# First expert stage of a small vision tower in slots of 64, as products on 64x64 quarters of TensorE

## The reference

```python
h = tokenizer(x)                                  # shifted patches, layer norm, one product
h = h + attention(layernorm(h))                   # 12 heads, quantised
h = h + ffn0(layernorm(h))                        # this stage is changed
h = h + ssm_block(layernorm(h))
h = h + ffn1(layernorm(h))                        # top 2 of 8 experts, hidden 768
```

```python
route = softmax(x @ router_w + router_b); e = argmax(route)
out[token] = (silu(x @ w1[e]) * (x @ w2[e])) @ w3[e]      # w1, w2: 192 x 512, w3: 512 x 192
out = out.astype(bfloat16) * max(route)
```

## Time and profile before

| quantity | value |
|---|---|
| median of 3 runs | 405.71 us |
| time of the profiled execution | 409.78 us |
| its span, first to last instruction | 408.0 us |
| mean granted clock of TensorE in it | 0.903 of 2.4 GHz |
| busy: PE, weight load, DVE, ACT, POOL | 85%, 71%, 45%, 33%, 26% |
| PE pieces of the first expert stage on the chain | 119.5 to 180.2 us |

### The profile page before, as it was taken

How to read it: one execution, slowest core, us unless ns; L and a number is a source line. 1 busy time by engine, 2 the same in 40 slices (tenths; PEclk the granted TensorE clock), 3 DMA queues, 4 the chain that set the end, 5 groups by cost and what they waited for, 6 DMA issues and landing times.

```text
span 408.0 us, 7081 instructions
## 1 busy us (share of the span) xinstructions
PE 348.6 (85%) x2758; PEld 291.5 (71%) x2758; DVE 184.0 (45%) x474; ACT 134.8 (33%) x278; POOL 104.5 (26%) x133
## 2 busy tenths in 40 slices
PE   4999946989788999966896987888899999999970
PEld 1999923567667999962465654575799999999960
DVE  2786793996552222216398555266422212121213
ACT  2997311444303222321387042321321212121210
POOL 3299542000023443122032202000423232211120
PEclk9999976987776999996999798995999999999995
DMA  7933239930371795007003999002249999999204
GB/s 237 345 84 75 63 81 253 271 93 2 108 202 52 203 247 124 15 16 195 0 0 77 258 252 259 28 0 67 60 105 291 277 254 255 258 251 249 65 31 130
DMA packets 28707, 59.51 MB, mean 146 GB/s; under 512 B 10081, under 2 KB 15234, under 8 KB 28674
## 3 DMA queue, kind: packets, MB, share of 16 engines
q1 hardware_dynamic: 26274, 53.48, 50.1%
q0 software_dynamic: 2400, 5.57, 5.0%
HBM read 55.12 MB, written 3.92 MB: 145 GB/s over the span
## 4 chain that ended last, share of the span: by engine, by line
PE 60%; DVE 17%; ACT 8%; DMA 8%; issue 4%; SPq 2%; POOL 0%; DVEq 0%; POOLq 0%; ACTq 0%
PE ps L1604 15%; PE ps L1629 12%; PE ps L1616 9%; PE ps L1412 4%; PE ps L1345 4%; DMA xw<-in_xw 3%; DVE cv L1264 3%; ACT xp L661 2%; PE ps L1418 2%; DVE xn L974 2%; DVE xn L950 2%; PE ps L1467 2%; SPq L349 2%; PE ps L1547 2%; DMA yg<-token_y 2%
## 5 line engine op out<-in xcount | busy, mean ns | idle before, releaser
L1604 PE MATMUL ps<-xgt,wup 128*128 128x128 f32 x576 | 70.9, 280 | 2.3 <-DVE ht L1196 1.8
L1604 PEld LDWEIGHTS ps<-xgt,wup 128*128 128x128 f32 x576 | 69.4, 196 | 2.8 <-issue 2.8
L1196 DVE TENSOR_TENSOR ht<-sg,ps 128x384 f32<-128x384 f32 (+1 forms) x56 | 27.7, 497 | 77.5 <-ACT sg L774 75.5
L597 POOL DMA_INDIRECT xg<-token_x,src_id x26 | 25.3, 972 | 145.5 <-DVE src_id L1166 95.3
L1629 PE MATMUL ps<-wdn,ht 128*128 128x192 f32 x288 | 53.8, 335 | 0.0
L1345 PE MATMUL ps<-busy 128*128 128x512 bf16 x108 | 38.9, 486 | 11.1 <-DVE h L1211 6.6
L1629 PEld LDWEIGHTS ps<-wdn,ht 128*128 128x128 f32 x288 | 46.1, 190 | 3.1
L604 POOL DMA_INDIRECT token_y<-ysb,row_id x28 | 27.5, 981 | 67.6 <-ACT ysb L781 67.6
L774 ACT ACTIVATE sg<-ps 128x384 f32<-128x384 f32 (+1 forms) x56 | 24.8, 444 | 49.9 <-PE ps L1616 49.1
L1353 PE MATMUL ps<-weff,xp 128*128 128x193 f32 x240 | 39.9, 327 | 1.6 <-ACT xp L661 1.6
L1353 PEld LDWEIGHTS ps<-weff,xp 128*128 128x128 f32 x240 | 39.2, 190 | 2.4 <-issue 2.4
(11 more groups left out here) (295 smaller groups left out, 511.0 us busy)
## 6 DMA issues: line engine op xcount, KB each, us to landing
wup<-in_m_w SPq DMA_DIRECT2D x16, 576.0 KB, 8.5
wup<-in_m_w SPq DMA_DIRECT2D x48, 192.0 KB, 9.4
wdn<-in_m_w SPq DMA_DIRECT2D x16, 576.0 KB, 11.4
wup<-in_m_w SPq DMA_DIRECT2D x12, 384.0 KB, 6.1
wup<-in_m_w SPq DMA_DIRECT2D x36, 128.0 KB, 6.6
wdn<-in_m_w SPq DMA_DIRECT2D x12, 384.0 KB, 9.3
xw<-in_xw SPq DMA_DIRECT2D x2, 784.0 KB, 12.3
wall<-in_w_sh SPq DMA_DIRECT2D x2, 768.0 KB, 10.2
```

Source lines behind the costliest of these rows:

```text
L597: g.indirect_dma_start(xg[:, j, :], None, token_x[m], bass.IndirectOffsetOnAxis(ap=src_id[:, j:j + 1], axis=0))\
L1196: v.tensor_tensor(ht[:, j % 2, s, 0:half], sg[:, s, 0:half], ps[:, 2 * s + 1, 0:half], ALU.mult)\
L1604: mm(ps[:, 2 * s + g, c * P:c * P + P], up[:, col:col + P], xgt[:, 0, j * P:j * P + P], start=(c == 0), stop=False)
```

## The change

The first expert stage now works in halves of 64 slots. An expert owns one half at least, and 16 halves (`M1_HALVES`) hold any routing: 8 static and 8 looked up. Two halves make one tile of 128 slots for the gather and the scatter, so there are 8 gathers' worth of tiles (`M1_TILES` is now 8) and 8 scatters. Weights are loaded for each half, so 16 times and not 12.

All products of the stage use 64x64 quarters of the array: the row half (partitions 0 to 63 or 64 to 127 of the operands) holds the gate matrix `w1` or the up matrix `w2`, the column half (partitions of the output) one of two blocks of 64 hidden units. For this the 192 channels stand as three blocks of 64 in both halves of the partitions (`xh`), and the weight buffer holds `w1` in partitions 0 to 63 and `w2` in 64 to 127. `across` transposes with 12 products of 64x64, `up_half` has 48 products for a half, `down_pair` 16 over 192 columns for both halves of a tile. The two row halves of `down_pair` write separate banks; ACT copies one to `y_low` and DVE adds the other (`both_rows`).

The weight loads are cut differently. `expert_weights` issues seven transfers: two that fill all 128 partitions from both matrices at once, through a source view that steps first over the matrix (g, two of them) and then over 64 rows, four pieces of 32 rows with 512 floats, and the down matrix as before.

```diff
+H = 64
+M1_HALVES = (T + E * (H - 1)) // H
+M1_TILES = (M1_HALVES + 1) // 2
+KB = D // H
-W_LOADS = 5
+W_LOADS = (7, 5)
...
+        y_low = sb("y_low", [P, D], scope=arena)
+        xh = xgt[:].rearrange("p m n -> p (m n)")[:, 0:2 * M1_TILES * D].rearrange("p (t k n) -> p t k n", k=KB, n=H)
...
-                sp.dma_start(up[0:DH, 0:2 * hid], w12[:, 0, :]).then_inc(S[f"d_wb{b}"], 16)
-                sp.dma_start(up[DH:P, 0:2 * hid], w12[0:lo, 1, :]).then_inc(S[f"d_wb{b}"], 16)
-                sp.dma_start(up[0:REM, 2 * hid:3 * hid], w12[lo:DH, 1, 0:hid]).then_inc(S[f"d_wb{b}"], 16)
-                sp.dma_start(up[REM:P, 2 * hid:3 * hid], w12[lo:DH, 1, hid:2 * hid]).then_inc(S[f"d_wb{b}"], 16)
+                if m == 0:
+                    def both(k):
+                        return up[:, k * hid:(k + 1) * hid]
+
+                    def gate_and_up(half, rows):
+                        return w12[rows, half, :].rearrange("p (g n) -> g p n", g=2)
+
+                    pieces = [(both(0), gate_and_up(0, slice(0, H))), (both(2), gate_and_up(1, slice(lo, DH)))]
+                    for g in range(2):
+                        at = H * g
+                        pieces += [(up[at:at + DH - H, hid:2 * hid], w12[H:DH, 0, g * hid:(g + 1) * hid]),
+                                   (up[at + DH - H:at + H, hid:2 * hid], w12[0:lo, 1, g * hid:(g + 1) * hid])]
...
+                for dst, src in pieces:
+                    sp.dma_start(dst, src).then_inc(S[f"d_wb{b}"], 16)
                 sp.dma_start(down[:], w3).then_inc(S[f"d_wb{b}"], 16)
...
-                for j in range(first, r["n"]):
+                for j in range(first, M1_HALVES if m == 0 else r["n"]):
                     if j == E:
                         sp.wait_ge(S["v_te"], m + 1)
-                    sp.wait_ge(S["p_y"], j - r["bufs"] + 1 + r["before"])
+                    last = j - r["bufs"]
+                    sp.wait_ge(S["p_y"], (last // 2 if m == 0 else last) + 1 + r["before"])
...
+                def both_rows(j):
+                    dve.wait_ge(S["a_yh"], j + 1)
+                    if j >= 2:
+                        dve.wait_ge(d_y[j % 2], j // 2 * 16)
+                    v.tensor_tensor(ysb[m][:, j % 2, :], y_low[:], ps[:, 5, 0:D], ALU.add).then_inc(S["v_y"], 1)
...
+                def across(j):
+                    pe.wait_ge(S[f"d_xg{j}"], rows_gathered(0, j))
...
+                    for c in range(KB):
+                        for s in range(2):
+                            rows = slice(H * s, H * s + H)
+                            for i in range(2):
+                                ins = mm(ps[H * i:H * i + H, 6 + s, c * H:c * H + H], xg[rows, j, H * c:H * c + H],
+                                         ident[rows, rows], start=True, stop=True)
+                    ins.then_inc(S["p_gt"], 2)
+
+                def up_half(j, s):
+                    t = 2 * j + s
...
+                    pe.wait_ge(S[f"d_wb{b}"], loads)
...
+                    for c in range(hid // P):
+                        for k in range(KB):
+                            for g in range(2):
+                                rows = slice(H * g, H * g + H)
+                                for i in range(2):
+                                    col = c * P + H * i
+                                    ins = mm(ps[H * i:H * i + H, 2 * s + g, c * H:c * H + H], up[rows, k, col:col + H],
+                                             xh[rows, t, k, :], start=(k == 0), stop=(k == KB - 1))
+                    ins.then_inc(S["p_gu"], 1)
+
+                def down_pair(j):
+                    pe.wait_ge(S["v_ht"], 2 * j + 2)
...
+                    for c in range(hid // P):
+                        for g in range(2):
+                            rows = slice(H * g, H * g + H)
+                            for i in range(2):
+                                dn = wbuf[0][(2 * j + i) % M1_BUFS][1]
+                                ins = mm(ps[H * i:H * i + H, 4 + g, 0:D], ht[rows, j % 2, i, c * H:c * H + H],
+                                         dn[rows, c, :], start=(c == 0), stop=(c == hid // P - 1))
+                    ins.then_inc(S["p_y"], 1)
+
+                if m_ == 0:
+                    for j in range(n):
+                        up_half(j, 0)
+                        if j >= 1:
+                            down_pair(j - 1)
+                        if j + 1 < n:
+                            across(j + 1)
+                        up_half(j, 1)
+                    down_pair(n - 1)
+                    return
```

More of the change, by code:

```diff
@@ L783, in experts @@
                 act.wait_ge(S["p_gt"], 2 * GROUPS[m] + 2)
-                a.copy(xgt[:, 0, 0:P], ps[:, 6, 0:P]).then_inc(S["a_gt"], 1)
-                for i in range(2):
-                    a.copy(xgt[REM * i:REM * i + REM, 1, 0:P], ps[REM:P, 7, 0:P]).then_inc(S["a_f1"], 1)
-                for j in range(n):
-                    if j == 0:
-                        gathered(1)
-                    elif j % 2 == 1 and j + 1 < n:
-                        gathered(j // 2 + 2)
-                    silu(j, 0)
-                    silu(j, 1)
-                    if j >= 1:
-                        result(j - 1)
+                if m == 0:
+                    first = ps[:, 6, 0:KB * P].rearrange("p (k t n) -> p t k n", k=KB, t=2)
+                    a.copy(xh[:, 0], first[:, 0]).then_inc(S["a_gt"], 1)
+                    a.copy(xh[:, 1], first[:, 1]).then_inc(S["a_f1"], 1)
+                    for j in range(n):
+                        silu(j, 0)
+                        if j >= 1:
+                            result(j - 1)
+                        if j + 1 < n:
+                            gathered(j + 1)
+                        silu(j, 1)
+                else:
+                    a.copy(xgt[:, 0, 0:P], ps[:, 6, 0:P]).then_inc(S["a_gt"], 1)
+                    for i in range(2):
+                        a.copy(xgt[REM * i:REM * i + REM, 1, 0:P], ps[REM:P, 7, 0:P]).then_inc(S["a_f1"], 1)
+                    for j in range(n):
+                        if j == 0:
+                            gathered(1)
+                        elif j % 2 == 1 and j + 1 < n:
+                            gathered(j // 2 + 2)
+                        silu(j, 0)
+                        silu(j, 1)
+                        if j >= 1:
+                            result(j - 1)
                 result(n - 1)
@@ L1076, in experts @@
                 r = MOE[m]
-                n, half, before, K = r["n"], r["hid"] // 2, r["before"], r["k"]
+                n, half, before, K, L = r["n"], r["hid"] // 2, r["before"], r["k"], r["slots"]
+                over = (M1_HALVES if m == 0 else n) - E
                 i_ln = 2 if m == 0 else 5
@@ L1197, in product @@
                         .then_inc(S["v_ht"], 1)
-                for j in range(n):
+                def both_rows(j):
[3 more added lines that the diff above has]
+                    v.tensor_tensor(ysb[m][:, j % 2, :], y_low[:], ps[:, 5, 0:D], ALU.add).then_inc(S["v_y"], 1)
+                for j in range(n):
+                    if m == 0:
+                        product(j, 0)
+                        if j >= 1:
+                            both_rows(j - 1)
+                        if j + 1 < n:
+                            gathered(j + 1)
+                        product(j, 1)
+                        continue
                     if j == 0:
@@ L1626, in down @@
                     if j >= 2:
[L1627 removed]
+                        pe.wait_ge(S["a_y"], j - 1)
                     for c in range(2 * tiles):
```

95 lines of the change are left out of this document (67 added, 28 removed).

## The result

The changed kernel takes 503.22 us (median of 4 runs, 502.28 to 504.24), the kernel before 405.79 us in the same job (4 runs, 405.24 to 407.61): a ratio of 1.239 with a 95% interval of 1.235 to 1.244, so 97 us slower. The profiled execution has a span of 500.6 us and took 502.28 us.

What follows compares the result with a forecast made beforehand. PE bounded the first expert stage before; after the change two DMA engines would: 57 + 204 + 5 us, then 5 us, end it at 271 instead of 180.2 us, +91 on the 405.7 us median, 497 us, range 470 to 600 us.

Steps and rivals of the forecast that it cites:

- The two engines: First expert stage's weight loads: two engines carry each 256 KB piece, 12.7 us an expert, 204 us for sixteen; chance 0.84.
- The order behind them: SP's queue: token stores, issued at 107.5 us behind six experts, land at 135 us, not 111; first gather waits for them.
- Products: PE in the first expert stage: eight pairs at 4.5 us, 36 us against 54 us, saving 18 us inside PE's idle time.
- The rival of 395 us: First expert stage: all engines share the pieces, the last pair ends at 170 us, 10 us less; 395 us, chance 0.11.
- the rival with slow quarters: First expert stage: small products cost 68 ns, a pair 8.4 us, with all engines sharing; +14 us, 420 us, chance 0.04.
- The signs: Stage profile: DMA share 0.12 to 0.15 at 45 to 50 GB/s; chain DMA, not PE; up products 1.6 us a half.
- The median: Whole kernel: 501 us against the profiled execution, less 4.1 us for its distance above the median, made 497 us.

Runs made afterwards that it cites:

- one piece: The changed kernel with the up matrices laid out in HBM as the buffer wants them, two transfers for an expert: 418.69 us, ratio 1.038.

## Why the prediction was right

**The two engines: right.** The term that decided was a source whose outermost count is two. 12.7 us per expert were worked out, 13.0 us are in the queue; the last weights landed at 268.8 us against 266; the stage ended at 275.5 against 271. The window at a share of 0.13 shows two busy engines. Cutting the pieces took 76 us away, merging two transfers in another stage of another kernel added 63. The Trainium skill, DMA: Bandwidth & Descriptors, section on why a DMA increments its semaphore by 16, gives this deal as its rule, and these three runs agree. The rate of 23.8 GB/s for a busy engine holds nearly, and is a mean of two: alone the two engines moved 24.5 each, 10.7 us for their 262 thousand bytes of an expert, which leaves 2.3 us for the shared 41 thousand, some 18 GB/s. Where the shared part is larger, as in the second stage above, 23.8 is too fast.

**The order behind them: right in kind, later by SP's own issues.** I had the token stores issued at 107.5 us and landing late, at 135 us. They were issued late, at 126.1 us, because SP stood in its own issues, and landed 10.5 us after the second issue, at 137. The step assumed that a queue takes what it is given. It cost next to nothing on top, since the last weights landed 2.8 us later than forecast.

**Products: hidden, as said, and their price came out by luck.** The 32 records of the 64x64 row are 16 products, so its 34 ns are the price of a record. I multiplied them by 124 products, each of which is two records; by that row a product costs 68 ns and a pair 8.4 us, which I had called the rival. But a record on four quarters starts every 15 ns at the full clock, less than half of the row's 34. The two errors cancel: a half's up products were forecast at 1.6 us and took 1.4, and a pair takes 4.5 us at the full clock (twice 1.4 us, 0.35 us of transposes, 1.3 us of `down`), the 4.5 of the forecast. What I had at nothing are the stops for instructions and the clock that falls with them: with one piece the eight pairs took 74 us, 21.4 of them stops, at a mean clock of 0.85, where 8 x 4.5 us are 36. The other 17 us are left to the lower clock and to gaps too short for the profile to call them idle; the runs don't part these two.

**The rival of 395 us: wrong in its sum.** It took shared pieces and cheap products for enough. The run that makes the pieces shared is at 427.6 us, the one that also makes them cheap to issue at 418.7. That the first lies near the 420 us of the rival with slow quarters is chance, as the quarters were not slow. The issue was readable ahead: seven to nine transfers at the 0.33 to 0.6 us of the earlier trace rows. The stops were not, in a kernel whose PE loads 22 blocks of instructions and shows no such stop in this stage. So even with every piece shared, none of the versions with quarters that compute everything was faster than the kernel before, and 0.11 for faster was too much.

**The signs.** The DMA share was forecast at 0.12 to 0.15 with 45 to 50 GB/s; it was 0.30 with 96. I had counted the work of the two engines and forgotten the other 640 KB of each expert: 1.18 MB in 13 us are 91 GB/s. Between the shared pieces the forecast figures stand there, 0.13 and 49. The landing of the 256 KB pieces isn't given in the trace. POOL's gather, PE's waits and the 1.6 us of the up products came as forecast. The chain is not PE, as forecast, but it is SP's queue (39%) more than DMA (4%).

**The median.** The sum against the profiled execution gave 501 us; I took 4.1 us off for the median of before and came to 497. Of the 6.2 us missed these 4.1 are the larger part; the stage ended 4.5 us later than forecast, what follows it was 2.7 us shorter, and the profiled execution lay 0.9 us below the median.

## What to carry to other kernels

Before a transfer is merged or reordered, read its source and its target from the outside in: the outermost count says over how many DMA engines it can be shared, and a count of two made 256 KB cost as much as 2 MB. A mean DMA share of 0.3 with a stalled issuing queue is the sign of it. When products are cut smaller, count instructions and not only products: on quarters the array kept the forecast pace, and with 16 blocks of instructions in place of 5 PE stood still for 21 of 74 us, longest where weights filled the DMA engines.

## What the runs showed of the hardware

- Two engines carry a transfer whose source has an outermost count of two: a DMA share of 0.13 with 49 GB/s between the shared pieces, 13.0 us per expert of 1.18 MB. SP's queue stands for 10 to 13 us in its issues meanwhile. How deep the queue is was not measured.
- With rows of 6 KB in one piece the 16 engines moved 328 to 423 GB/s in full slices of the stage, against 222 to 280 with the pieces of the kernel before.
- On 64x64 quarters with 64 columns a record of an f32 product starts every 15 ns at the full clock and every 26 ns at 0.50, and with 32 columns the kernel is no faster.
- PE's instructions come in blocks of 16 KB (33 packets for 8512 instructions). In the kernel with one piece stops stood 127 products and 127 weight loads apart; they took 2.8 to 3.8 us at a DMA share of 0.88 to 0.99 and 1.0 to 1.6 us at 0.01 or less.
- A record with 128x128 weights takes 111 ns with 128 columns and 116 ns with 64. With 64x128 weights and 64 columns it takes 55 to 60 ns.
- PE busy for 18.00 of 18 us was granted 0.50 in two windows in a row with 64x128 weights (126 to 162 us); what lifts or holds the clock there stays open.
